# Narrow expert jobs of the first half ahead of the second half's dispatch, and an attention bias carried as three bf16 rows

## The reference, cut to what matters

```python
h = layernorm(x) * (1 + ca) + sa
x = x + ga * (silu(q @ W1 + b1) @ W2 + b2)          # W1, b1, W2, b2 come out of the scan
h = layernorm(x) * (1 + cb) + sb
# ffn: 8 experts, the best 2 of each token, and one shared expert
acc = gelu(h @ Ws1.T + bs1) @ Ws2.T + bs2
acc = acc + sum over the token's 2 experts of gate * (gelu(h @ W1[e].T + b1[e]) @ W2[e].T + b2[e])
x = x + gb * SCALE * acc
```

## Time and profile before

| | |
|---|---|
| median of 3 executions | 533.71 us (533.15 to 535.95) |
| the profiled execution, its own time | 532.91 us |
| span of the profile | 531.1 us, mean granted clock 0.971 |
| scan | to about 265 us |
| first dispatch on POOL | 292.8 us |
| first expert matmul | 349.5 us |
| end of the last matmul | 519.0 us |

### The profile page before, as it was taken

How to read it: one execution, slowest core, us unless ns; L and a number is a source line. 1 busy time by engine, 2 the same in 40 slices (tenths; PEclk the granted TensorE clock), 3 DMA queues, 4 the chain that set the end, 5 groups by cost and what they waited for, 6 DMA issues and landing times.

```text
span 531.1 us, 13354 instructions
## 1 busy us (share of the span) xinstructions
PE 486.6 (92%) x4030; PEld 442.3 (83%) x4030; DVE 390.8 (74%) x1613; ACT 365.6 (69%) x1383; POOL 349.4 (66%) x521
## 2 busy tenths in 40 slices
PE   3699999999999999999899979899989999899790
PEld 2489999999999999999747769789979998899680
DVE  4688888888898888988678887427885663343864
ACT  3369999899999999999759588554444544555450
POOL 4257767676776767775320788888888888776640
PEclk9579999999999999999998999999999999999997
DMA  9999900000000000000000114545447788698876
GB/s 194 332 397 393 354 3 1 2 1 3 2 2 2 2 2 2 2 2 2 1 2 0 43 42 134 182 120 172 129 134 217 244 269 260 215 286 265 329 231 184
DMA packets 39277, 68.50 MB, mean 129 GB/s; under 512 B 7475, under 2 KB 25781, under 8 KB 39205
## 3 DMA queue, kind: packets, MB, share of 16 engines
q1 hardware_dynamic: 31764, 56.69, 33.4%
q0 software_dynamic: 4320, 8.99, 4.8%
q10 hardware_dynamic: 3120, 1.97, 1.3%
HBM read 38.16 MB, written 29.46 MB: 127 GB/s over the span
## 4 chain that ended last, share of the span: by engine, by line
PE 62%; POOL 16%; issue 6%; DVE 6%; DMA 5%; ACT 3%; SPq 2%; another core or an unknown queue 1%; POOLq 0%; ACTq 0%; DVEq 0%
PE bank L1418 35%; POOL xs L1287 12%; PE bank L671 8%; PE bank L685 8%; POOL rested L1276 4%; DMA xr<-in_L_attn_x_dram 1%; PE bank L653 1%; DMA xt<-xs 1%; ACT hid L805 1%; DMA yg<-ys 1%; PE bank L566 1%; SPq L217 1%; PE bank L1627 1%; PE bank L1504 1%
## 5 line engine op out<-in xcount | busy, mean ns | idle before, releaser
L1295 POOL DMA_INDIRECT ys<-yo,dst x71 | 71.6, 1008 | 30.9 <-issue 15.2
L1287 POOL DMA_INDIRECT xs<-hrow,slot_i x64 | 62.9, 984 | 38.0 <-issue 38.0
L805 ACT ACTIVATE hid<-bank,slab 128x256 f32<-128x256 f32 (+1 forms) x172 | 62.6, 443 | 29.9 <-PE bank L671 23.0
L685 PE MATMUL bank<-slab,hid 128*128 128x128 f32 x568 | 71.9, 276 | 2.9 <-issue 1.6
L685 PEld LDWEIGHTS bank<-slab,hid 128*128 128x128 f32 x568 | 69.5, 192 | 5.4 <-issue 1.8
L671 PE MATMUL bank<-hg,slab 128*128 128x256 f32 (+1 forms) x344 | 68.8, 343 | 0.5 <-ACT hg L813 0.5
L671 PEld LDWEIGHTS bank<-hg,slab 128*128 128x128 f32 x344 | 55.0, 191 | 5.2 <-issue 0.7
L1174 DVE TENSOR_TENSOR yb<-bank,slab 128x256 f32<-128x256 f32 (+1 forms) x43 | 16.2, 378 | 56.2 <-PE bank L685 32.8
L813 ACT COPY hg<-bank 128x256 f32<-128x256 f32 (+1 forms) x43 | 14.4, 338 | 49.6 <-PE bank L653 34.4
L1276 POOL MEMSET rested<- 128x1408 f32 x32 | 41.3, 1290 | 0.0
L2311 POOL TENSOR_TENSOR nH<-aH,ones 128x128 f32<-128x128 f32 x32 | 14.9, 466 | 33.8 <-ACT aH L1767 33.8
(11 more groups left out here) (423 smaller groups left out, 1809.3 us busy)
## 6 DMA issues: line engine op xcount, KB each, us to landing
slab<-in_slabs_dram SPq DMA_DIRECT2D x43, 578.0 KB
xs<-fill SPq DMA_DIRECT2D x34, 528.0 KB, 7.6
xt<-xs SPq DMA_DIRECT2D x28, 132.0 KB
yg<-ys SPq DMA_DIRECT2D x7, 512.0 KB, 5.8
out_dram<-xr SPq DMA_DIRECT2D x18, 64.0 KB
ys<-yo,dst POOLq DMA_INDIRECT x71
xr<-in_L_attn_x_dram SPq DMA_DIRECT2D x4, 256.0 KB, 6.6
xs<-hrow,slot_i POOLq DMA_INDIRECT x64
```

Source lines behind the costliest of these rows:

```text
L685: mm = pe.matmul(y[:, s * D:(s + 1) * D], hid[i % 2][:, n, s * P:(s + 1) * P], right, start=(n == 0), stop=(n == FT - 1), skip_group_check ...
L805: nc.scalar.activation(hid[i % 2][:, n, 0:w], e_half(i, n)[:, 0:w], ACT.Gelu_apprx_tanh, bias=bias).then_inc(e_x, 1)
L1287: pool.indirect_dma_start(out=xs[:, :], out_offset=bass.IndirectOffsetOnAxis(ap=slot_i[:, i, c:c + 1], axis=0), in_=hrow[:, c, :], in_offs ...
L1295: pool.indirect_dma_start(out=ys[:, :], out_offset=bass.IndirectOffsetOnAxis(ap=dst[v][:, s:s + 1], axis=0), in_=yo[v][:, s, :], in_offset ...
```

## The change

Seven narrow tiles are taken forward: with 9 wide tiles and 7 narrow ones, 25 units are sure to hold rows of the first half, and all 16 tiles now stand ahead of the wait for `s_half[1]`. There are 25 wide and 21 narrow tiles in place of 28 and 15 (71 units, as before), and 53 jobs. Three shared pieces that stood among the first jobs move behind them, and three, not two, stand at the end. New functions `early_halves` and `begin_rest` compute the tables of the early narrow tiles and what is left over behind them. The loads of `yg` of groups 0 to 3 move behind all loads of rows and weights, and `SUMS` moves into the last jobs. `yo` has 18 buffers in place of 10; for the room, the early shared pieces use the tiles `hid` of the jobs in place of their own. The bias b2 becomes three bf16 rows (head, middle and rest) in `b2t`, made by 7 small DVE instructions, and one bf16 matmul of 3 rows adds it; the copy to `hrow` moves behind `spread(0)`.

```diff
+RW = 5
+FULL_HALVES = -(-(B * S - E * (P - 1)) // P) - SUB * N_FULL      # 7
+N_EARLY = N_FULL + FULL_HALVES                                   # 16
-N_WHOLE = (2 * B * S // P - E) // 2                              # 28
-N_HALF = (2 * B * S + E * (P - 1)) // P - 2 * N_WHOLE            # 15
+N_REST = 16
+N_WHOLE = N_FULL + N_REST                                        # 25
+N_HALF = (2 * B * S + E * (P - 1)) // P - SUB * N_WHOLE          # 21
-ORDER = "WW.WW.WW.WW.W." + "WWWW" + 6 * "WH" + 2 * "WWH" + "WWWWW" + "HHHHHHH" + ".."
+ORDER = "WW.WWWWHWHWHWHH.HH" + "WWW" + 4 * "WH" + "." + 4 * "WH" + "WWWWW" + "." + "HHHHHH" + "..."
-RY = 10
+BIASED, BIAS_AT = EARLY_SH + 2, 19
+RY = 18
...
             sp.wait_ge(s_half[0], 16 * CH)
-            for j in range(N_FULL):
+            for j in range(N_EARLY):
+                if j == EARLY_HALF:
+                    sp.wait_ge(table_ready, 4)
                 rows(j)
                 if j >= RW:
                     weights(j)
-            sp.wait_ge(table_ready, 4)
-            weights(N_FULL)
-            weights(N_FULL + 1)
+            sp.wait_ge(table_ready, 6)
+            weights(N_EARLY)
+            weights(N_EARLY + 1)
             sp.wait_ge(s_half[1], 16 * CH)
-            for j in range(N_FULL, N_TILES):
+            for j in range(N_EARLY, N_TILES):
                 rows(j)
...
-                if j == LOAD_AT:
-                    scattered(sp, BY_HALF)
-                if LOAD_AT <= j < LOAD_AT + 4:
-                    load(sp, j - LOAD_AT)
+            scattered(sp, BY_HALF)
+            for g in range(4):
+                load(sp, g)
             scattered(sp, BY_THREE)
...
-                    pe.wait_ge(b2_ready, 1)
-                    pe.matmul(bank[2 + g % 2][:, :], ones[0:1, :], b2r[:, :], start=True, stop=False, skip_group_check=True)
+                    pe.wait_ge(b2_ready, 7)
+                    pe.matmul(bank[2 + g % 2][:, :].rearrange("p (c d) -> p c d", c=GRP), onesq[0:3, :],
+                              b2t[:, :].unsqueeze(1).broadcast_to([3, GRP, D]), start=True, stop=False, skip_group_check=True)
...
-            SUMS = {-12: (0, 1), -11: (2, 3), -10: (4, 5), -9: (6,), -8: (7,), -7: (8,), -6: (9,), -5: (10,), -4: (11,), -3: (12, 13, 14, 15), -2: (16,)}
+            SUMS = {-5: (0,), -4: (1, 2, 3, 4, 5), -3: (6, 7, 8, 9, 10, 11), -2: (12, 13, 14, 15, 16, 17)}
...
-                if i == 2:
+                if i == 0:
+                    early_halves()        # 16 small instructions
+                elif i == 1:
+                    begin_rest()          # 6
+                elif i == 3:
                     rest_marks()
-                elif i == 3:
+                elif i == 4:
                     ends(marks)
-                elif i == 5:
+                elif i == 6:
                     experts_of(rest, n_rest)
-                elif i == 6:
-                    rows_at(rest, n_rest, marks, TS, 3)
                 elif i == 8:
+                    rows_at(rest, n_rest, marks, TS, 5)
+                elif i == 9:
                     half_marks()
-                elif i == 9:
+                elif i == 10:
                     ends(marksh)
-                elif i == 11:
-                    experts_of(halves, N_HALF)
                 elif i == 12:
-                    rows_at(halves, N_HALF, marksh, P, 5)
+                    experts_of(halves, N_HALF - N)
+                elif i == 13:
+                    rows_at(halves, N_HALF - N, marksh, P, 7)
```

More of the change, by code:

```diff
@@ L419, in program @@
         first, rowf = psb("first", [P, N_TILES]), psb("rowf", [P, N_TILES])
-        hs = [psb(f"hs{i}", [P, FT, SH]) for i in range(2)]
         ysh = [psb(f"ysh{i}", [P, SUB, D]) for i in range(2)]
@@ L1060, in tail_vector, with early_halves @@
             over_all = spare[:, 0:V * U].rearrange("p (v k) -> p v k", v=V)
             over_by = spare[:, 0:V * U].rearrange("p (v k o) -> p v k o", v=V, o=2)
+            def early_halves():
+                seen = past[:, 0:N, :]
+                then(dve.tensor_reduce(full_by[:, :], over[:, :, :], AX_X, ALU.add))
+                then(dve.tensor_scalar(begun[:, :], marks[:, 0:E], float(SUB), None, ALU.mult))
+                then(dve.tensor_tensor(full[:, :], full_by[:, :], begun[:, :], ALU.subtract))
+                then(dve.tensor_tensor(tri[:, 0:E, :], full[:, :].unsqueeze(1).broadcast_to([P, E, E]),
+                                       cut["tri"].rearrange("p (a b) -> p a b", b=E), ALU.mult))
+                then(dve.tensor_reduce(last[:, 0, :], tri[:, 0:E, :], AX_X, ALU.add))
+                then(dve.tensor_tensor(seen, cut["tile"][:, 0:N].unsqueeze(2).broadcast_to([P, N, E]),
+                                       last[:, 0, :].unsqueeze(1).broadcast_to([P, N, E]), ALU.is_ge))
+                then(dve.tensor_reduce(etab[:, early], seen, AX_X, ALU.add))
+                dve.tensor_scalar(e_i[:, early], etab[:, early], float(E - 1), None, ALU.min).then_inc(table_ready, 1)
+                then(dve.tensor_tensor(weight[:, 0:E - 1], full_by[:, 0:E - 1], begun[:, 1:E], ALU.subtract))
+                then(dve.tensor_copy(weight[:, E - 1:E], full_by[:, E - 1:E]))
+                then(dve.tensor_tensor(seen, seen, weight[:, 0:E].unsqueeze(1).broadcast_to([P, N, E]), ALU.mult))
+                then(dve.tensor_reduce(first[:, early], seen, AX_X, ALU.add))
+                then(dve.tensor_tensor(rowf[:, early], cut["tile"][:, 0:N], first[:, early], ALU.subtract))
+                then(dve.tensor_scalar(rowf[:, early], rowf[:, early], begun[:, 0:1], float(P), ALU.add, ALU.mult))
+                then(dve.scalar_tensor_tensor(out=rowf[:, early], in0=etab[:, early], scalar=float(CAP), in1=rowf[:, early],
+                                              op0=ALU.mult, op1=ALU.add))
+                dve.wait_ge(table_ready, 3)
+                dve.tensor_copy(row_i[:, early], rowf[:, early]).then_inc(table_ready, 1)
@@ new lines, in begin_rest @@
+            def begin_rest():
+                then(dve.tensor_scalar(last[:, 0, :], last[:, 0, :], float(N), None, ALU.min))
+                then(dve.tensor_tensor(begun[:, 1:E], begun[:, 1:E], last[:, 0, 1:E], ALU.add))
+                then(dve.tensor_tensor(begun[:, 1:E], begun[:, 1:E], last[:, 0, 0:E - 1], ALU.subtract))
+                then(dve.tensor_tensor(begun[:, 0:1], begun[:, 0:1], last[:, 0, 0:1], ALU.add))
+                then(dve.tensor_scalar(marks[:, 0:E], begun[:, :], 1.0 / SUB, None, ALU.mult))
+                then(dve.scalar_tensor_tensor(out=left[:, :, :], in0=begun[:, :].unsqueeze(1).broadcast_to([P, 3, E]), scalar=-float(P),
+                                              in1=held[:, :, :], op0=ALU.mult, op1=ALU.add))
@@ L1071, in rest_marks @@
                 dve.wait_ge(turned, NG)
[L1072 removed]
+                then(dve.tensor_tensor(over_all, left[:, :, :].rearrange("p k e -> p (k e)").unsqueeze(2).broadcast_to(grid),
                                        cut["step"].unsqueeze(1).broadcast_to(grid), ALU.is_gt))
```

70 lines of the change are left out of this document (44 added, 26 removed).

## The result

| | before | after |
|---|---|---|
| median (4 executions each) | 534.12 us (533.15 to 535.95) | 540.28 us (539.72 to 542.07) |
| ratio | | 1.0098, 95% interval 1.0062 to 1.0135 |
| profiled execution, span | 532.91, 531.1 | 539.72, 537.9 |
| first expert matmul | 349.5 | 355.2 |
| first expert matmul to the end of the last matmul | 169.5 | 169.0 |

The kernel became 1.0% slower; 529.8 was forecast, with a range of 525.5 to 536.5. Between the two profiled spans lie 6.8 us: +5.7 until the first expert matmul, -0.5 in the jobs, +1.6 in the tail. The forecast had -0.4, -4.3 and +0.8.

What follows compares the result with a forecast made beforehand. The last third was taken as PE's work, 12.8 us that PE loses, and a 12.1 us tail. Start -0.4, work +0.15, losses -4.4 and tail +0.8 gave -3.9, so a median of 529.8 us, range 525.5 to 536.5.

Steps and rivals of the forecast that it cites:

- Part 1: Bias at the start: cheaper PE matmuls against seven chained DVE instructions; -0.4 us at the first expert matmul (+0.9 to -1.5).
- rival C: DVE becomes the bound in jobs 8 to 14, some instructions held by POOL; 537.8 us, chance 0.15.
- Part 2: PE work of the jobs with the new numbers of wide and narrow tiles: +0.15 us.
- Part 3: PE's wait at the dispatch, tile 16, rows behind SP's weights of tile 17: 1.3 us in place of 2.1 (0 to 4).
- Parts 4 and 5: DVE's table work between first jobs: 0 more; seven early narrow tiles: +1.0 (0 to 4.0); eight late pairs: 4.1.
- late pairs: Eight late pairs of narrow and wide tiles: PE's loss stays at 4.1 us (2 to 7).
- Part 6: Last narrow run: PE's loss falls from 5.9 to 1.2 us (0 to 4), `yg` loads now behind all weights.
- Part 7: Tail behind PE's last matmul: 13.1 in place of 12.1, set by DVE's group steps; +0.8 us taken (-2 to +2).
- Rival B: Every narrow tile costs PE what it costs now, 0.48 us each, in early and late stretches; 533.7 us, chance 0.25.

Runs made afterwards that it cites:

- c_before: The kernel before, unchanged, run for a trace on the chip of the experiments; its single execution took 530.87 us.
- c_after: The kernel after, unchanged, run again beside the kernel before on a chip of the experiments; 533.36 us, 1.0043 of the kernel before.
- e5: The kernel after with float32 bias matmuls behind a chain of seven DVE instructions; 534.97 us, 1.0053 of the kernel before.
- e3_filled_again: The kernel after with three float32 matmuls that nothing reads in PE's gap; 542.16 us, beside 547.26 for the kernel after, unchanged.
- batch 2: Second set of runs on one chip, kernel before beside them at 530.93 us; kernel after 1.0043, kernel before with the new bias alone 1.0046.
- batch 4: Fourth set of runs, kernel before beside them at 538.32 us; on the first set's chip, some 25 minutes apart; kernel after 1.0225.
- e1_old_bias_again: The kernel after with the bias of the kernel before, run a second time on the same chip; 547.06 us, 1.0186 of the kernel before.
- e10: The kernel after with SP issuing the weights of tile 17 behind the rows of tile 16; 546.43 us, 1.0147 of the kernel before.
- e1_old_bias: The kernel after with the bias of the kernel before (float32 row, two DVE copies), first run; 530.12 us, 0.9997 of the kernel before.
- e4_short_chain: The kernel after with one DVE copy for the seven-instruction chain, leaving out two bias parts; 527.87 us, 0.9944 of the kernel before.
- e8: The kernel after with the three bias rows made on POOL in place of DVE; 529.64 us, 0.9966 of the kernel before.

## Why the prediction was wrong

**The step that failed is Part 1**, the sum at the first expert matmul: -0.4 us with bounds +0.9 and -1.5, measured +5.7 in the first traces and +3.1 between c_before and c_after. Three things in it:

- The chain was taken as 7 x 0.32 = 2.2 us, and was 3.7. The 0.29 is right, or nearly so, for five of the seven (0.28 to 0.34); one cast took 0.78 and the subtraction with both inputs in SBUF 1.25, beside POOL's two additions. In e5, where the same cast ran wholly beside the second addition, it took 1.29. The row of 2.25 was used for rival C's place and not for this one, where POOL was at work as well. The Trainium skill, page "SBUF — State Buffer", section "Who interferes with whom", says that a DVE instruction with two inputs in SBUF contends with a GpSimd instruction that reads SBUF, and that one with a single SBUF input does so only if it is a copy, a cast or a `tensor_scalar` in a mode that takes both port pairs. The trace agrees: 1.25 at L1238 against 0.28 at L1236, whose other input is in PSUM, and 0.78 for the cast at L1237.
- "5.0 us less on PE, little of it is on the path" was right, and the other side of it was missing: work that is taken from PE ahead of a wait becomes idle time. PE was done with group 3 1.6 us sooner, ACT began the rows that it needs next 1.8 later (280.34 instead of 278.57), and so PE stood for 2.32 us.
- The price of that idle time. Behind it the granted clock is 0.50, from 284.5 on for 13.7 us and again for 3.4 near 312; before, it was 0.50 for 3.4 us from 288.4. Routing took 3.42 instead of 1.85 us. Filled with useless work, the same gap gave 5.1 us back (e3_filled_again). That the clock is what makes the difference is shown by that pair; how much of the 5.7 in the first trace is clock and how much is lateness was not separated for that execution. The Trainium skill, page "TensorE: Matmul & The Clock Gate", section "Part 1: The HAM clock gate (the "warmup" mystery)", has the two levels and that an idle PE falls to the lower one. The granted clock here is never anything but 0.50 or 1.00, and the falls behind PE's gaps agree; the fall below, with PE busy, does not, and there the measurement decides.

The size is not a constant: the bias alone costs 0.46% in batch 2, and old against new bias 0.3% in batch 4 (547.06 and 548.59, with intervals that overlap; at least 0.4% was expected). The clock also falls without a gap. In e1_old_bias_again, with the old bias and the short chain, PE was busy for 18.15 of the 18.30 us before the fall and all through it:

```profile
267.00:285.30 18.30, 18.15 (x84) 10.16 (x82) 14.97 (x59) 12.30 (x25) 2.69 (x4) 1.00 0.01 2
285.30:295.50 10.20, 10.20 (x46) 8.03 (x46) 7.08 (x32) 7.02 (x19) 0.72 (x1) 0.50 0.00 0
```

So the gap makes the fall likelier or longer, as the filled gap shows, and is not its only cause. What brings it about in this trace stays open.

**Part 2** (+0.15): right as far as the rows show; in the last narrow run DVE's rows come every 1.90 us, as forecast for a narrow job.

**Part 3** (a wait of 1.3 at tile 16, between 0 and 4): right in kind and place, SP behind the weights of tile 17; its size was 2.79, and 2.8 to 5.5 in the others whose SP queue has that order. The term was mis-sized by 1.5 us. In c_after the clock was at 0.50 for 3.4 us from 409.4, beside this wait; the step had no term for that. e10 adds what the step did not see: moving the load only moves the wait.

**Parts 4 and 5** (0 beyond part 3, and +1.0 for early narrow tiles, between 0 and 4): from 355.1 to 410.2 PE was idle 2.7 us, and the fifteen jobs took 4.7 us over their work. Under the upper bound, over the value taken. That the same kernel spends 49.8 or 54.05 us there was not foreseen at all. The late pairs lost 3.3 us of idle time, where 4.1 was taken.

**Part 6** (5.9 becomes 1.2): right, and it was 0. In all, the jobs gave 0.5 us where 4.3 were forecast: what part 6 gained was lost again at tile 16 and in the early stretch.

**Part 7** (+0.8, tail 13.1): 13.7 in the first trace, 13.0 to 13.3 in the others. DVE sets the end, as forecast; the 0.79 for the load of group 6 behind the stores of groups 0 and 2 is what was not read from SP's order.

Sum of the errors: 6.1 + 3.8 + 0.8 = 10.7 us, which is the distance of the spans (527.2 forecast, 537.9). Part 1 alone turns the forecast gain into a loss of 2.2 us and stays in the range (529.8 + 6.1 = 535.9); with the 3.8 of the jobs the result is outside it.

Rival B had the jobs nearer (0.15 less 0.6 is -0.45, where -0.5 was measured), but by luck: it charged every narrow tile 0.48 us, and the last narrow run lost nothing, while tile 16 and the early stretch lost more. Rival C had the contention with POOL, at another place, and its 537.8 is the nearest of the four by luck as well: its sign was DVE at 0.95 from 375 to 400, and DVE was busy 19.73 of those 25 us (0.79). None had the clock. One reading of the prediction is loose and changes nothing: the shares 2.1, 4.1 and 5.9 of what PE lost are called proportional to the idle times 1.81, 2.86 and 4.48, and are so only roughly.

**What stays open.** Why releases come late in some executions, and why the new order is then 1.0 to 1.9% slower while the kernel before loses less. Narrow jobs, with twice as many hand-overs between PE, ACT and DVE per microsecond, standing ahead of jobs that DVE shares with its tables, is an argument and was not tried by itself. Single traces point the same way and do not carry the sizes: from the first expert matmul to the end of the last one, the new order has 163.4 to 166.2 us in six traces without such waits, against 167.4 and 170.5 for the old one, and where there are such waits 169.0 to 176.2 in eight traces against 169.1, 169.5, 171.7 and 173.1.

## What to carry to other kernels

Before work is taken off PE, look at what PE waits for next: if that is another engine, the saving becomes idle time, and behind idle time the clock of what followed was halved here, so an edit that is neutral on the path can cost microseconds. Small chained instructions should be put on an engine that is idle there, and priced by the rows beside which they will run, not by their like elsewhere. Where a stage runs with two-deep buffers and several engines, measure a new order more than once, with time between: 0.9997 and 1.0186 are both true of one kernel on one chip here.

## What the runs showed of the hardware

- Useless matmuls made a kernel faster: about 3 us of them gave 5.1 us (547.26 to 542.16).
- The clock fell to 0.50 for 10.2 us at 285.3 in e1_old_bias_again, behind 18.30 us of which PE was busy 18.15.
- Beside an addition of POOL, a cast of 3 x 128 elements on DVE took 0.78 and 1.29 us and a subtraction 1.25, with all inputs in SBUF; with an input in PSUM either took 0.28.
- Between 280 and 320 us the clock was at 0.50 for no time at all in e1_old_bias and e4_short_chain and for 20 us in c_after. In c_before one fall of 10.2 us lies at 296.7, where the first trace of the same kernel has none: it is not fixed by the program alone.
- One kernel (e1) against one other (before) gave 0.9997, 1.0103 and 1.0186, with the kernel before at 531.1, 533.8 and 538.3 us; the first and the last are of one chip.
- On POOL the same small operations are slower than on DVE: a scaling of 3 x 128 took 0.59 to 1.11 us in e8, on DVE 0.28; a subtraction 0.42 against 0.28.
